# Two half sums of a sampled tile: added by accumulating transposes instead of by VectorE

## The reference

```python
om = conv3x3(x, offset_w) + offset_b           # 18 offsets and 9 mask logits per position
pos_y, pos_x = base + tap + offset             # 9 taps, clipped
v1, v2, v3, v4 = x at the four corners of (pos_y, pos_x)
value = (hh * hw * v1 + hh * lw * v2 + lh * hw * v3 + lh * lw * v4) * mask
value = value.reshape(N, oH, oW, C * 9)
out = einsum('nhwc,cf->nhwf', value, w)        # 576 -> 64 channels
```

## Time and profile before

| | us |
|---|---|
| median of 3 runs | 4096.59 |
| lowest, highest | 4096.07, 4101.5 |
| the profiled execution's own time | 4098.25 |
| its span, first to last instruction | 4096.4 |
| TensorE, matmuls busy | 3461.7 (85%) |
| VectorE busy | 3031.0 (74%) |
| ScalarE busy | 2169.1 (53%) |
| GpSimd busy | 1998.3 (49%) |

### The profile page before, as it was taken

How to read it: one execution, slowest core, us unless ns; L and a number is a source line. 1 busy time by engine, 2 the same in 40 slices (tenths; PEclk the granted TensorE clock), 3 DMA queues, 4 the chain that set the end, 5 groups by cost and what they waited for, 6 DMA issues and landing times.

```text
span 4096.4 us, 57899 instructions
## 1 busy us (share of the span) xinstructions
PE 3461.7 (85%) x21240; PEld 1861.4 (45%) x21240; DVE 3031.0 (74%) x4876; ACT 2169.1 (53%) x3704; POOL 1998.3 (49%) x1805
## 2 busy tenths in 40 slices
PE   5979997999899999999899999999899999946431
PEld 2434444444544445444544455444544454525321
DVE  6466477877688687877688678878688678855775
ACT  5744774467545774467545774467545764422210
POOL 0000064654466364655466464646466465757760
PEclk9989998999899999999899989999899989955555
DMA  4022124441354334442343334432343324534355
GB/s 113 1 62 71 47 82 117 138 121 55 88 148 129 79 87 119 138 110 61 102 142 115 81 96 124 140 94 71 106 143 107 81 82 138 148 102 125 94 127 110
DMA packets 446955, 419.18 MB, mean 102 GB/s; under 512 B 327249, under 2 KB 364369, under 8 KB 446545
## 3 DMA queue, kind: packets, MB, share of 16 engines
q0 software_dynamic: 85248, 231.33, 19.2%
q1 hardware_dynamic: 361424, 184.17, 18.0%
HBM read 381.93 MB, written 59.30 MB: 108 GB/s over the span
## 4 chain that ended last, share of the span: by engine, by line
PE 61%; DVE 17%; ACT 9%; DVEq 5%; issue 4%; DMA 2%; SPq 1%; POOL 1%; ACTq 0%
PE PS L1571 54%; PE PS L1769 3%; DVE work L939 3%; DVEq L525 3%; DVE G L529 2%; DVE G L523 2%; PE PS L1605 2%; DVE small L935 1%; ACT work L1462 1%; ACT xn_stacks L1309 1%; ACT token_cm L1309 1%; ACT work L1391 1%; POOL G L485 1%; ACT small L1436 1%; PE PS L1609 1%
## 5 line engine op out<-in xcount | busy, mean ns | idle before, releaser
L485 POOL DMA_INDIRECT G<-corner_table,index x1800 | 1997.7, 1110 | 1964.6 <-DVE index L741 671.8
L1462 ACT ACTIVATE work<-PS,descale 128x512 f32<-128x512 f32 (+2 forms) x896 | 567.2, 633 | 872.2 <-PE PS L1571 861.6
L1391 ACT ACTIVATE work<-PS 128x768 f32<-128x768 f32 (+2 forms) x800 | 651.7, 823 | 276.9 <-PE PS L1571 231.4
L851 DVE TENSOR_TENSOR work<-work 128x768 f32<-128x768 f32 (+2 forms) x496 | 480.1, 972 | 302.2 <-PE PS L1571 253.0
L1571 PE MATMUL PS<-token_cm,xn_stacks 128*128 128x400 f16 (+3 forms) x3200 | 630.4, 339 | 47.6 <-ACT work L1391 38.4
L939 DVE TENSOR_TENSOR work<-PS,work 128x512 f32<-128x512 f32 (+2 forms) x896 | 551.4, 619 | 142.0 <-ACT work L1462 132.8
L1571 PE MATMUL PS<-work,xm 128*64 128x400 f32 (+3 forms) x3200 | 622.3, 501 | 0.0
L523 DVE TENSOR_TENSOR G<-G,corner_w 128x768 f32<-128x768 f32 x600 | 561.8, 951 | 49.8 <-DMA G<-corner_table,index 48.7
L1571 PEld LDWEIGHTS PS<-token_cm,xn_stacks 128*128 128x128 f16 (+1 forms) x3200 | 286.5, 100 | 463.1 <-ACT work L1391 180.7
L1571 PE MATMUL PS<-work,w3s 128*64 128x384 f32 (+2 forms) x1792 | 439.1, 568 | 67.7 <-DVE small L935 67.7
L1571 PE MATMUL PS<-token_cm,w1h 128*128 128x512 f16 (+2 forms) x896 | 318.2, 355 | 57.9 <-DVE work L939 51.6
(11 more groups left out here) (253 smaller groups left out, 4283.3 us busy)
## 6 DMA issues: line engine op xcount, KB each, us to landing
G<-corner_table,index POOLq DMA_INDIRECT x1800
corner_table<-rows_scratch SPq DMA_DIRECT2D x32, 784.0 KB
small<-share_scratch SPq DMA_DIRECT2D x192, 128.0 KB
small<-share_scratch SPq DMA_DIRECT2D x192, 96.0 KB
share_extra<-share_scratch SPq DMA_DIRECT2D x96, 128.0 KB
om_cm<-share_scratch SPq DMA_DIRECT2D x96, 128.0 KB
share_extra<-share_scratch SPq DMA_DIRECT2D x96, 96.0 KB
om_cm<-share_scratch SPq DMA_DIRECT2D x96, 96.0 KB
```

The costliest lines, as they stand in the source:

```text
L485: GP.indirect_dma_start(G[0:rows, n % 2, tap * 4 * C:(tap + 1) * 4 * C], None, tables[b % 2], bass.IndirectOffsetOnAxis(ap=index[0:rows, c ...
L851: V.tensor_tensor(sq[0:rows, u % 4, :, 0:n], relu[0:rows, u % 2, :, 0:n], relu[0:rows, u % 2, :, 0:n], ALU.mult).then_inc(s["sq_dve"], 1)
L1391: A.activation(relu[0:rows, u % 2, :, 0:n], PS[u % 2][0:rows, :, 0:n], ACT.Relu).then_inc(s["relu_done"], 1)
L1462: A.activation(silu[:, e % 2, 0:w], S[e % 2][:, 0:w], ACT.Silu, scale=descale[:, MOE1:MOE1 + 1]).then_inc(s["silu_done"], 1)
```

## The change

VectorE's second sum (piece 4) goes. Its first sum (piece 3) now writes to `values`, which is twice as wide: the half sums of corners 0 + 2 of all taps, and behind them those of corners 1 + 3. It takes over the wait for `val_tr` and the signal `valued`, so this is raised at step 6 of a mixer group in place of 7, and at expert 5 of eight in place of 7. Each transpose in `sample` becomes two into the same columns of PSUM, the second of which adds: ten per tile in place of five.

```diff
@@ -166,7 +166,7 @@
         G = sb("G", [128, 2, 4 * TAPS * C])
         stage, stage2 = G[:, 0, :], G[:, 1, :]
         stage3 = work
-        values = sb("values", [TP, 2, TAPS * C])
+        values = sb("values", [TP, 2, 2 * TAPS * C])
         val_cm = sb("val_cm", [128, 5 * TP])
         dcn_cm = sb("dcn_cm", [128, TP])
         share = (small_flat[:, 0:512], small_flat[:, 512:1024], share_extra[:, :], om_cm[:, :])
@@ -523,13 +523,10 @@
                     V.tensor_tensor(g, g, bc(w, 2, C), ALU.mult)
                 else:
                     dve.drain()
-                    if piece == 4 and b * T + t > 1:
+                    if b * T + t > 1:
                         dve.wait_ge(s["val_tr"], 2 * (b * T + t - 1))
-                    if piece == 3:
-                        V.tensor_tensor(g[:, :, 0:2, :], g[:, :, 0:2, :], g[:, :, 2:4, :], ALU.add)
-                    else:
-                        V.tensor_tensor(values[:, q, :].rearrange("p (n c) -> p n c", n=TAPS), g[:, :, 0, :], g[:, :, 1, :],
-                                        ALU.add).then_inc(s["valued"], 1)
+                    V.tensor_tensor(values[:, q, :].rearrange("p (s n c) -> p n s c", n=TAPS, s=2), g[:, :, 0:2, :], g[:, :, 2:4, :],
+                                    ALU.add).then_inc(s["valued"], 1)
 
             def sample_add(b, t):
                 dve.wait_ge(s["dcn_done"], b * T + t + 1)
@@ -859,7 +856,7 @@
                                 sample_add(k - 2, late_tile(j))
                             if k >= 1 and half and 1 <= jh < FULL and u == MIX_ADD:
                                 sample_add(k - 1, jh - 1)
-                            for piece in range(5):
+                            for piece in range(4):
                                 if k >= 2 and j < NLATE - 1 and MIX_WEIGH[piece] == u:
                                     weigh(k - 2, late_tile(j) + 1, piece)
                                 if k >= 1 and half and jh < FULL and MIX_WEIGH[piece] == u:
@@ -1015,8 +1012,6 @@
                     weigh(k - 1, FULL, 3)
                 for q in range(2, 4):
                     split_l("a", k, 0, q)
-                if k >= 1:
-                    weigh(k - 1, FULL, 4)
                 gate(k)
                 if k >= 2:
                     ffn_bias(k - 2)
@@ -1596,17 +1591,25 @@
 
                 n = b * T + t + 1
                 value = values[:, (n - 1) % 2, :]
+
+                def turned(bank, tap, start, stop):
+                    for half in range(2):
+                        at = (half * TAPS + tap) * C
+                        ins = P.matmul(bank, value[:, at:at + 2 * C], ident[0:TP, 0:TP], start=start and half == 0, stop=stop and half == 1,
+                                       is_transpose=True, skip_group_check=True)
+                    return ins
+
                 if stage == 0:
 
                     pe.wait_ge(s["valued"], n)
                     if n > 1:
                         pe.wait_ge(s["conv_added"], n - 1)
                     for i in range(4):
-                        ins = P.transpose(D0[:, i * TP:(i + 1) * TP], value[:, i * 128:(i + 1) * 128], ident[0:TP, 0:TP])
+                        ins = turned(D0[:, i * TP:(i + 1) * TP], 2 * i, True, True)
                     ins.then_inc(s["val_tr"], 1)
                 if stage == 1:
                     pe.wait_ge(s["val_ready"], n * 2 - 1)
-                    P.transpose(D0[:, 0:TP], value[:, 7 * C:9 * C], ident[0:TP, 0:TP])
+                    turned(D0[:, 0:TP], TAPS - 2, True, True)
                     for i in range(4):
                         h, weight, product = i % 2, dcn[:, i, :], val_cm[:, i * TP:(i + 1) * TP]
                         if token_form(b, t):
```

## The result

| | before | after |
|---|---|---|
| median of the runs | 4097.6 us (4096.07 to 4101.5) | 4167.51 us (4161.89 to 4171.65) |
| profiled execution, own time | 4098.25 | 4161.89 |
| its span | 4096.4 | 4160.1 |

The ratio is 1.0166, with a 95% interval of 1.0153 to 1.018: the changed kernel is 1.7% slower. The forecast was 4180 us, 2.0% slower, with 4142 to 4212 as the range. The profiled execution shown here is the fastest of the four.

A forecast was written before the change was run, and what follows sets the result against it. TensorE, busy 85% and 61% of the chain, was taken as the bound. 14 + 13 + 7.6 + 38 + 10.9 = 83.5 us on 4098.25 gave 4181.8, stated as 4180 us for the median; range 4142 to 4212.

The forecast's parts named there:

- The direction and the main mechanism: Whole kernel: slower, since work moves to the busier TensorE, each added transpose costing 0.11 us at full clock; slower given 0.91.
- Rival 3: Transposes: the second of a pair waits for the first one's write, 1.35 us a tile, 4310 us; chance 0.04.
- rival 4: VectorE's sum: the strided write costs a second pass, about 25 us more, 4205 us; chance counted within the forecast's 0.87.
- rivals 1 and 2: Experts: 1, TensorE absorbs transposes, VectorE's relief counts, 4085 us, chance 0.05; 2, gains and costs cancel, 4097 us, chance 0.04.
- Experts: Experts, 7 times: 7.7 us of transposes less 2.6 of VectorE relief for images 1 to 6, full 7.7 for the last: +38.
- which leaves 2.6 for VectorE: Experts: of the last image's 5.1 us less TensorE idle time, table loads explain 2.6, the other 2.6 credited to VectorE's relief.
- First halves: First mixer halves, 6 times: TensorE's chain takes in four of five tiles' transpose groups and all single ones, 2.3 us each: +14.
- Second halves: Second mixer halves, 7 times: three of the groups of four transposes and all five single ones in the chain, 1.9 us each: +13.
- Gate: Gate, 7 times: one tile transposed at half clock in the chain, +1.08 us each, VectorE's sum hidden: +7.6 us.
- Tail: Tail, tiles 0 to 24: transposes cost 1.08 us at half clock, rounds 0.25 or 1.08 longer, less sums of 0.83: +10.9.
- The share of weight loads: Rule against the forecast: weight loads busy 45% leave TensorE over half free, VectorE is busiest, so the change would pay.

The follow-up runs named there:

- e2: The kernel before, both VectorE sums kept, each of its five transposes followed by an accumulating one of zeros: 4179.94 us, ratio 1.0193.
- e3: The changed kernel, with the second transpose of each pair overwriting what the first wrote instead of adding to it: 4171.08 us, ratio 1.0166.
- again: The changed kernel timed and profiled a second time, nothing changed: 4167.37 us, ratio 1.0158.
- e7: The changed kernel with filler matmuls of zeros in the tail, ahead of most tiles and late feed-forward chunks: 4161.68 us, ratio 1.0154.
- e4: The changed kernel with its one sum moved to the old second sum's place (step 7 in mixers, expert 7): 4165.53 us, ratio 1.017.
- e10: The changed kernel, but the 98 tiles sampled in the experts keep two sums and five transposes: 4139.52 us, ratio 1.0096.
- e1: The changed kernel with only the first half sums transposed: one strided sum, five transposes a tile, corners 1 and 3 left out: 4078.92 us, ratio 0.9943.
- e6: The kernel before with filler matmuls of zeros in the tail, ahead of most tiles and late feed-forward chunks: 4098.37 us, ratio 0.9999.
- e8: The kernel before with its first sum moved in the experts from expert 5 to 7, right ahead of the second: 4151.26 us, ratio 1.0129.
- e9: The kernel before with its first sum moved in the experts from expert 5 to 6: 4205.65 us, ratio 1.0259.
- e5: The kernel before with its first sum cut in two by taps, at experts 5 and 6 (both at step 6 in mixers): 4110.67 us, ratio 1.0028.

## Why the prediction was right, step by step

**The direction and the main mechanism** hold. The cost is a TensorE cost (e2 has it without any change on VectorE), it is 0.11 us per transpose at full clock (rows above), and the strided sum costs what the plain one did. Rival 3 (the adding write waits) is excluded by e3 and by the step of 0.22 us for a pair; rival 4 (a second pass for the strided write) by the 1358 ns; rivals 1 and 2 by the experts' +43.6 and +46.0 us.

**A correction for the clock** is needed before single terms can be compared. Four transposes of `values` step 0.44 us at full clock and 0.87 at half, so of the time that a busy TensorE spends at half clock half is lost. The time at half clock differs from trace to trace. The table gives for each stage the shift against before, the time at half clock (before: 21, 62 and 17 us, and 179 in the gate), and the shift corrected by half of the difference (9.0 + 11 / 2 = 14.5). In the gate TensorE waits too much for that. The last three kernels have the same code as before in all stages but those left empty here, so their rows show what moves by itself.

| shift, at half clock: corrected | first halves | second halves | experts | gate |
|---|---|---|---|---|
| after | 9.0, 10: 14.5 | 7.3, 57: 9.8 | 43.6, 14: 45.1 | 4.8, 188 |
| again | 10.3, 12: 14.8 | 4.8, 50: 10.8 | 46.0, 20: 44.5 | 0.9, 179 |
| e7 (fillers in the tail) | 10.3, 12: 14.8 | 7.2, 56: 10.2 | 45.1, 17: 45.1 | 8.0, 190 |
| e3 (no adding) | 10.1, 11: 15.1 | 4.5, 41: 15.0 | 46.4, 20: 44.9 | 12.5, 204 |
| e4 (late sum) | 11.2, 15: 14.2 | 8.7, 64: 7.7 | 31.4, 3: 38.4 | 14.2, 200 |
| e10 (experts old) | 12.2, 16: 14.7 | 11.2, 64: 10.2 | -0.6, 14: 0.9 | 12.1, 199 |
| e2 (TensorE's part) | 9.5, 10: 15.0 | 8.2, 49: 14.7 | 44.2, 14: 45.7 | 12.1, 202 |
| e1 (VectorE's part) | 0.8, 22: 0.3 | -8.9, 46: -0.9 | -0.9, 20: -2.4 | 1.6, 186 |
| e6 (before, fillers in the tail) | 0.1, 21: 0.1 | -1.8, 59: -0.3 | -0.6, 14: 0.9 | 0.2, 179 |
| e8 (sum at expert 7) | -5.9, 7: 1.1 | -3.3, 51: 2.2 | | 7.6, 201 |
| e9 (sum at expert 6) | -1.6, 17: 0.4 | 1.9, 64: 0.9 | | -1.4, 177 |

This is worked out from the traces; no run held the clock fixed. But the last three rows bear it out in the first halves, where shifts of -5.9 to +0.1 us of the same code come to 0.1 to 1.1.

**Experts: predicted +38, measured +43.6 and +46.0. The step that failed is "which leaves 2.6 for VectorE".** It read the shorter idle time of the last image as the worth of its lighter VectorE. e1 gave VectorE nearly the same relief in images 1 to 6 and won 0.9 us in seven images (2.4 corrected), where 6 x 2.6 = 15.6 had been expected. The last image differs from the others in more than VectorE's load, and I had no right to give the whole rest to that one difference. What else makes up its shorter idle time stays open. An error the other way hid much of it: I let the transposes cost their full 7.7 us, but images 1 to 6 paid 5.0 to 6.8 in the first trace and 5.0 to 6.7 in the second (9.3 for its image 1), with 6.2 and 6.6 as the means over all seven. The count of the steps explains half of that, 14 x 0.49 = 6.9 us, because a few tiles hide their new transposes in a wait for a product (0.99 us became 0.60). So the price per image was 7.7 less about 1.4 that TensorE's own waits take in, with or without VectorE's relief (e2), where I had written 7.7 less 2.6 for that relief. The last image, predicted at 7.7, got 7.2 and 7.1.

**First halves: predicted +14, measured +9.0 and +10.3.** The count of the chain was right, and the size is off by the clock, as far as the traces can say: corrected, the seven traces with ten transposes a tile lie between 14.2 and 15.1, which leaves nothing for VectorE.

**Second halves: predicted +13, measured +7.3 and +4.8.** Here VectorE's relief and the clock are mixed. TensorE's part alone (e2) comes to 14.7 when corrected, and the changed kernel to 9.8, 10.8 and 10.2 (after, again, e7), so the relief would be worth 4 to 5; but e3 has the same relief and stands at 15.0, so that value isn't sure. How much of the missing 6 to 8 us is clock and how much is VectorE stays open.

**Gate: predicted +7.6, measured +4.8 and +0.9**, and +8.0 to +14.2 in the other traces with ten transposes. A gate of images 2 to 7 lasts 42 to 50 us over all traces, the longer the more time at half clock is in it (19 to 35 us), and the same code as before gives -1.4 to +7.6 us (e9, e8). The 1.08 us that were read from the chain are inside that scatter: the term is neither confirmed nor refuted.

**Tail: predicted +10.9, measured +1.0 and +9.8.** The rounds came as written, +0.2 and +1.1 by turns and 6.5 us in all (1.75 + 5.4 = 7.15 predicted), and e1 and e2 show both terms behind them, 0.83 and 1.07, by themselves. Tiles 3 to 7 were 5.0 us longer at half clock (`again`; 5.4 - 0.83 = 4.6 predicted) and 3.9 shorter where half of them ran at full clock. The prediction took 1.2 GHz throughout, as the earlier trace rows show it before, and made no allowance for a stretch of 2.4 GHz; what brought it, the runs don't show. In e3, e4 and e10, which have the same work in the tail, it is 6.8, 6.4 and 9.1 us longer.

**In the sum** the errors have both signs: the experts 6 to 8 us too low, mixers, gate and tail together 20 to 23 too high. The result lies 12.5 us below the forecast, well inside the range; that it came so close is in part luck, since these errors cancel. The added transposes cost 0.11 us each in line, with TensorE's weight loads busy 47% of the span. The Trainium skill (Perfetto Trace Analysis, Identifying the Most-Contended Engine) would have TensorE's headroom judged by FLOPs and by the weight loads' share, not by matmul busy time. The share of weight loads, by which TensorE would have been half free, misled in this kernel; the FLOPs were not counted.

## What to carry to other kernels

Price an added short matmul by the step between starts in the stage where it lands, and look for its cover at that very place: in the experts TensorE, idle for 16 us of 206, hid about 1.4 of the 7.7 us that it was given. Relief of the other engine is worth only what hangs behind the instruction that was removed; a stage that differs in several ways is no measurement of it, and a kernel that has the relief alone is (e1: 10 us less of work in a stage, 0.2 us less of time). Where two engines pass tiles to and fro in every step, try the place of a long instruction by itself, since moving one sum by one expert (e9) cost more than this whole change.

## What the runs showed that I had not expected

- Moving one 1.36 us sum from expert 5 to 6 costs 112 us over the experts stages, 16 us an image; in image 3 nearly half of it is the same matmuls at a lower granted clock (0.95 for 0.99), beside 9.5 us more of idle time on TensorE. The seven stages had 99 us at half clock, 17 before.
- Matmuls of zeros kept the tail's clock up in part (392 us at half clock in place of 492), and won 2.0 us of the tail in the kernel before, more in the changed one.
- Stages whose code is the same as before moved by -5.9 us (first halves, e8) and +7.6 us (gate, e8), along with their time at half clock.
- The gate stages of one program differ by up to 6.5 us from image to image (e2, images 2 to 7: 43.6 to 50.1), the longest with the most time at half clock (35 us, against 25).
- Of the kernels that do all the work, none was faster than the kernel before. The nearest are e6 (0.9999) and e5 (1.0028).
